# A three-pass down projection, rows loaded by SyncE, and another seam order in a fused decoder layer on one core

## What is computed

```python
x = x + self_attention(layernorm(x))             # 16 heads, window of 64
x = x + cross_attention(layernorm(x), ctx)       # 16 heads, relative bias
xf = layernorm(x)
probs = softmax(xf @ router_w.T); topv, topi = top_k(probs, 2)
g = einsum('nd,edf->nef', xf, gate_w) + gate_b   # F = 512
u = einsum('nd,edf->nef', xf, up_w) + up_b
h = silu(g) * u
y = einsum('ne,ned->nd', probs, einsum('nef,efd->ned', h, down_w) + down_b)
x = x + y
```

## Time and profile before

| | |
|---|---|
| median of 3 runs (lowest to highest) | 1213.61 us (1212.24 to 1214.14) |
| the profiled execution's own time | 1211.85 us |
| its span, first to last instruction | 1210.2 us |
| mean granted TensorE clock | 0.989 |
| busy: PE, DVE, ACT, POOL | 97%, 72%, 62%, 68% of the span |
| DMA | 86.11 MB, mean 71 GB/s |

### The profile page before, as it was taken

How to read it: one execution, slowest core, us unless ns; L and a number is a source line. 1 busy time by engine, 2 the same in 40 slices (tenths; PEclk the granted TensorE clock), 3 DMA queues, 4 the chain that set the end, 5 groups by cost and what they waited for, 6 DMA issues and landing times.

```text
span 1210.2 us, 36900 instructions
## 1 busy us (share of the span) xinstructions
PE 1168.2 (97%) x12874; PEld 1023.7 (85%) x12874; DVE 868.3 (72%) x3851; ACT 753.8 (62%) x1845; POOL 821.0 (68%) x1593
## 2 busy tenths in 40 slices
PE   6899999999999999999999999999899999999996
PEld 4688888888888888888888888887689999998995
DVE  3567888888888888888888888888777655544442
ACT  2567766767766767766766766766564555555552
POOL 4677788778788778788778788876636644444432
PEclk8999999999999999999999999999899999999998
DMA  8411122121122121112112112122765433333221
GB/s 191 93 43 47 50 59 75 50 58 58 51 58 75 50 58 58 51 59 75 52 58 59 51 58 71 48 65 87 230 212 140 76 57 54 53 58 56 46 32 23
DMA packets 70936, 86.11 MB, mean 71 GB/s; under 512 B 25600, under 2 KB 57728, under 8 KB 70752
## 3 DMA queue, kind: packets, MB, share of 16 engines
q1 hardware_dynamic: 54768, 58.60, 16.7%
q0 software_dynamic: 15552, 25.05, 10.7%
q10 hardware_dynamic: 432, 0.10, 0.0%
HBM read 43.10 MB, written 20.95 MB: 53 GB/s over the span
## 4 chain that ended last, share of the span: by engine, by line
PE 90%; DVE 4%; issue 2%; POOL 2%; DMA 1%; ACT 0%; POOLq 0%; DVEq 0%
PE bank_S L901 10%; PE bank_Q L824 7%; PE bank_P L824 6%; PE bank_Q L916 5%; PE bank_S L815 5%; PE bank_S L866 5%; PE bank_B L737 4%; PE bank_A L737 4%; PE bank_B L837 4%; PE bank_A L837 3%; PE bank_A L804 3%; PE bank_P L763 3%; PE bank_B L804 3%; PE bank_Q L876 3%; PE bank_B L796 3%; PE bank_S L754 3%
## 5 line engine op out<-in xcount | busy, mean ns | idle before, releaser
L628 POOL TENSOR_SCALAR arena<-arena,mC 112x375 f32<-112x375 f32 x512 | 297.6, 594 | 26.4 <-DVE mC L1282 24.3
L1282 DVE CUSTOM_DVE_ANT_0 arena<-bank_S,arena 112x375 f32<-112x375 f32 x512 | 260.4, 543 | 56.9 <-PE bank_P L824 30.4
L634 POOL TENSOR_SCALAR arena<-arena 112x112 f32<-112x112 f32 x512 | 175.0, 356 | 85.3 <-DVE arena L1270 85.3
L654 POOL DMA_INDIRECT out<-y,xb x63 | 106.6, 1692 | 83.8 <-DVE y L1420 48.6
L824 PE MATMUL bank_Q<-ident,arena 112*126 112x112 f32 x858 | 131.9, 262 | 2.1 <-POOL arena L628 1.5
L1071 ACT ACTIVATE pTC<-bank_P 126x336 f32<-126x336 f32 x226 | 102.6, 454 | 40.6 <-PE bank_P L824 16.9
L1270 DVE CUSTOM_DVE_ANT_0 arena<-bank_S,arena 112x112 f32<-112x112 f32 x512 | 102.1, 270 | 14.6 <-PE bank_S L754 14.6
L1071 ACT ACTIVATE pTC<-bank_Q 126x336 f32<-126x336 f32 x222 | 101.3, 456 | 18.1 <-PE bank_Q L824 14.6
L824 PEld LDWEIGHTS bank_Q<-ident,arena 112*126 112x126 f32 x858 | 96.2, 141 | 15.4 <-issue 9.7
L824 PE MATMUL bank_P<-ident,arena 112*126 112x112 f32 x678 | 107.9, 268 | 1.3 <-ACT pTC L1071 0.8
L647 POOL DMA_DIRECT2D xb<-xs x63 | 44.1, 700 | 80.1 <-issue 76.6
(11 more groups left out here) (263 smaller groups left out, 3566.9 us busy)
## 6 DMA issues: line engine op xcount, KB each, us to landing
arena<-in_l_ctxT SPq DMA_DIRECT2D x32, 378.0 KB, 3.5
k<-k_low SPq DMA_DIRECT2D x64, 188.0 KB, 2.3
xb<-xs POOLq DMA_DIRECT2D x63, 129.0 KB
q<-q SPq DMA_DIRECT2D x64, 112.0 KB
arena<-in_L_ffn_gate_w SPq DMA_DIRECT2D x8, 512.0 KB
arena<-in_L_ffn_up_w SPq DMA_DIRECT2D x8, 512.0 KB
arena<-in_L_ffn_down_w SPq DMA_DIRECT2D x8, 512.0 KB
arena<-in_x SPq DMA_DIRECT2D x32, 112.0 KB, 2.0
```

Source lines behind the costliest of these rows:

```text
L628: pool.tensor_scalar(z[n % NZ][:, 0:T], z[n % NZ][:, 0:T], -1.0, mC[:, n:n + 1], ALU.mult, ALU.add).then_inc(s_u, 1)
L634: m = pool.tensor_scalar(sF[r][:, j, :], sF[r][:, j, :], -1.0, mF[:, r, j:j + 1], ALU.mult, ALU.add)
L654: pool.indirect_dma_start(out=out[:, :], out_offset=bass.IndirectOffsetOnAxis(ap=xb[x][:, D + 1:D + 2].bitcast(I32), axis=0), in_=y2[x % 2 ...
L1282: dve.tensor_tensor_reduce(out=z[n % NZ][:, 0:T], in0=bank[f"S{r}"][0:S, 0:T], in1=nbias[:, n, :], scale=1.0, scalar=3.0e38, op0=ALU.add, ...
```

## The change

The down projection of the pairs is now done in three passes of fp32r. ScalarE makes the high parts of the hidden rows (`hidden_high`) and of the down weights (`weights_high(..., "dw", ...)`) ahead of silu in step `bg`, VectorE the low parts (`hidden_low`, `weights_low`) at the end of its part of `bg`. `hidden_rows` has one buffer instead of two, `xb` 10 instead of 12. The weighted sums of a pair go alternately into `y2` and `xbT`, so there are four buffers for them up to the last three pairs. The rows of all blocks are loaded by SP (`load_rows`, `load_behind`), not by POOL. In `TAIL_ORDER` only packages 0 to 3 stand at the head, packages 4 to 15 behind the `get` steps, of which there are 8 instead of 10; the parts of the block table come earlier, and `pv3 oc3` ahead of `x3T x3Tc`.

```diff
-XB = 12
+XB = 10
...
 TAIL_ORDER = """
-pkg:0 pkg:1 pkg:2 pkg:3 pkg:4 pkg:5 pkg:6 pkg:7 pkg:8 pkg:9 v0 ln3:-2 t14:-1 st:-2 rs3:-2 t13:-1 p8:-1 v0c
...
-p10 u14 rcA:-2 e10 p9 get:0 u15 e9 p14 u13 x3:-1 pv1 get:1 u12 get:2 get:3 get:4 get:5 get:6 get:7 get:8 get:9
-p15 e14 warm pv2 oc1 e15 p13 oc2 p12 e13 pf:-2 e12 pkg:10 pkg:11 pkg:12 pkg:13 pkg:14 pkg:15 pfD:-2 rcB:-2
-x3T:-1 x3Tc:-1 pv3 oc3 bt otc nrmc rt:-1 lg:-1 re:-1 sc:-2 bg:0 bt:1 onC oncc rcA:-1 bu:0 woc bg:1 st x2 ln3 rs3
...
+pkg:0 pkg:1 pkg:2 pkg:3 v0 ln3:-2 t14:-1 st:-2 rs3:-2 t13:-1 blocks:0 p8:-1 v0c p11:-1 t12:-1 pv0:-1 t15:-1
...
+e6 u10 st:-1 ln3:-1 p8 u9 p11 t14 pv0 rs3:-1 t13 t12 e8 oc0 t15 e11 p10 u14 rcA:-2 e10 p9 get:0 get:1 u15 e9 p14
+u13 x3:-1 pv1 get:2 get:3 u12 get:4 get:5 get:6 get:7 p15 e14 warm pv2 oc1 e15 p13 oc2 p12 e13 pf:-2 e12 pkg:4
+pkg:5 pkg:6 pkg:7 pkg:8 pkg:9 pkg:10 pkg:11 pkg:12 pkg:13 pkg:14 pkg:15 pfD:-2 rcB:-2 pv3 oc3 x3T:-1 x3Tc:-1 bt
+otc nrmc rt:-1 lg:-1 re:-1 sc:-2 bg:0 bt:1 onC oncc rcA:-1 bu:0 woc bg:1 st x2 ln3 rs3 pf:-1 pfD:-1 rcB:-1 sc:-1
+bu:1 x3 x3T x3Tc bg:2 add:0 add:1 rt lg re bu:2 rcA bg:3 add:2 add:3 pf pfD rcB sc blocks:5 bu:3 blocks:6 bg:4
...
-                  for w, n, m in (("gw", DC, F), ("uw", DC, F))}
+                  for w, n, m in (("gw", DC, F), ("uw", DC, F), ("dw", FC, D))}
+            hR = [sb(f"hR_{part}", [P, FC, 2 * P], F32R, st) for part in ("high", "low")]
+            rows_out = [[y2[h] if k % 2 == 0 or k > NP - 4 else xbT[h] for h in range(2)] for k in range(NP)]
...
@@ SP
+                    def load_rows(j):
+                        r = sp.value_load(blocks[0:1, 0, j:j + 1], min_val=0, max_val=E * R)
+                        sp.dma_start(xb[j % XB][:, :], xs[bass.ds(r, P), :]).then_inc(s_xb[j % XB], 16)
+
+                    def load_behind(j):
+
+                        if j:
+                            sp.wait_ge(s_add, 16 * (j - (j > NFULL)))
+                        for n in (j + XB - 2, j + XB - 1) if j < NFULL else (j + XB - 2,):
...
+                            if n < NBLK:
+                                load_rows(n)
...
+                        elif step == "get":
+                            if b == 0:
+                                sp.wait_ge(s_blocks, 1)
+                                buffers_free(sp)
...
+                            load_rows(b)
+                        elif step == "add" and b % 2 == 0:
+                            load_behind(b)
...
@@ PE
                     def down_pair(k):
-                        e = expert_of(pe, 2 * k)
-                        pe.wait_ge(s_hh, 2 * k + 2)
+                        pe.wait_ge(s_dw, k + 1)
+                        pe.wait_ge(s_hl, k + 1)
                         if k:
                             pe.wait_ge(s_yw, 2 * k)
-                        w = package(e, "dw").rearrange("p (c d) -> p c d", c=FC)
                         for h in range(2):
                             for c in range(FC):
-                                m = pe.matmul(bankY[:, h * D:(h + 1) * D], hidden_rows[k % 2][:, c, h * P:(h + 1) * P], w[:, c, :],
-                                              start=(c == 0), stop=(c == FC - 1))
+                                for u, w in PASSES:
+                                    m = pe.matmul(bankY[:, h * D:(h + 1) * D], hR[u][:, c, h * P:(h + 1) * P],
+                                                  wR["dw"][w][:, c, :], start=(c == 0 and (u, w) == PASSES[0]),
...
@@ ACT
+                    def hidden_high(k):
+                        act.wait_ge(s_hh, 2 * k + 2)
+                        if k:
+                            act.wait_ge(s_y, 2 * k)
+                        act.activation(hR[0][:, :, :], hidden_rows[:, :, :], ACT.Copy).then_inc(s_hi, 1)
...
                         elif step == "bg":
...
+                            if b:
+                                hidden_high(b - 1)
+                                weights_high(b - 1, "dw", s_y)
                             for half in range(2):
                                 silu_pair(b, half)
...
@@ DVE
+                        if j >= NFULL:
+                            dve.wait_ge(s_add, 16 * max(j - 1, NFULL))
+                        elif j // 2 > NP - 3:
+                            dve.wait_ge(s_add, 16 * (j - j % 2))
+                        elif j >= 4:
+                            dve.wait_ge(s_add, 16 * (j - j % 2 - 2))
...
+                    def hidden_low(k):
+                        dve.wait_ge(s_hi, k + 1)
+                        dve.tensor_tensor(hR[1][:, :, :], hidden_rows[:, :, :], hR[0][:, :, :].bitcast(F32),
+                                          ALU.subtract).then_inc(s_hl, 1)
...
+                            if b:
+                                hidden_low(b - 1)
+                                weights_low(b - 1, "dw", s_dw, 1)
```

More of the change, by code:

```diff
@@ L518, in load_bias @@
                             sp.dma_start(nbias[s0:s0 + SK, HG * g:HG * (g + 1), :], skewed).then_inc(s_nb[g], 16)
+                    def load_rows(j):
[5 more added lines that the diff above has]
+                        for n in (j + XB - 2, j + XB - 1) if j < NFULL else (j + XB - 2,):
+                            if n == 2 * NP1:
+                                sp.wait_ge(s_blocks, 2)
+                                for q in range(2):
+                                    need(sp, s_st[q], 16 * (B // 2))
+                                    need(sp, s_sc[q], 32 * (B // 2))
+                            if n == NFULL:
+                                sp.wait_ge(s_blocks, 3)
+                                sp.wait_ge(s_pad, 16 * E)
+                                sp.wait_ge(s_spare, 16)
+                            if n < NBLK:
+                                load_rows(n)
                     load_x(0)
@@ L583, in _ @@
                             load_package(sp, e, half)
+                        elif step == "get":
+                            if b == 0:
+                                sp.wait_ge(s_blocks, 1)
+                                buffers_free(sp)
+                                for q in range(2):
+                                    need(sp, s_sc[q], 32 * ((B1 + 1 - q) // 2))
+                                    need(sp, s_st[q], 16 * ((B1 + 1 - q) // 2))
+                            load_rows(b)
+                        elif step == "add" and b % 2 == 0:
+                            load_behind(b)
+                    for j in range(1 + max(b for step, b in steps if step == "add"), NBLK):
+                        if j >= NFULL or j % 2 == 0:
+                            load_behind(j)
                     sp.wait_ge(s_add, 16 * NBLK)
@@ L643, in scatter @@
                                 in_=x3[b % 2][k][:, :], in_offset=None).then_inc(s_sc[b % 2], 16)
-                    def load(j, x):
-                        r = pool.value_load(blocks[0:1, 0, j:j + 1], min_val=0, max_val=E * R)
-                        pool.dma_start(xb[x][:, :], xs[bass.ds(r, P), :]).then_inc(s_xb[x], 16)
                     def add(j, x):
@@ L700, in _ @@
                             scatter(b)
-                        elif step == "get":
-                            if b == 0:
-                                pool.wait_ge(s_blocks, 1)
-                                buffers_free(pool)
-                                for q in range(2):
-                                    need(pool, s_sc[q], 32 * ((B1 + 1 - q) // 2))
-                                    need(pool, s_st[q], 16 * ((B1 + 1 - q) // 2))
-                            load(b, b)
                         elif step == "add":
-                            add_and_load(b)
+                            add(b, b % XB)
                         elif step == "pad":
@@ L1119, in weights_high @@
                             act.wait_ge(used, 2 * k)
-                        act.activation(wR[part][0][:, :, :], package(e, part).rearrange("p (c f) -> p c f", c=DC), ACT.Copy).then_inc(s_wh[part], 1)
+                        act.activation(wR[part][0][:, :, :], package(e, part).rearrange("p (c f) -> p c f", f=parts[part][1] // (
+                            FC if part == "dw" else DC)), ACT.Copy).then_inc(s_wh[part], 1)
                     def silu_pair(k, half):
@@ L1430, in weights_low @@
                         dve.wait_ge(s_wh[part], k + 1)
-                        dve.tensor_tensor(wR[part][1][:, :, :], package(e, part).rearrange("p (c f) -> p c f", c=DC), wR[part][0][:, :, :].bitcast(F32), ALU.subtract).then_inc(then, n)
+                        dve.tensor_tensor(wR[part][1][:, :, :], package(e, part).rearrange("p (c f) -> p c f", f=parts[part][1] // (
+                            FC if part == "dw" else DC)), wR[part][0][:, :, :].bitcast(F32), ALU.subtract).then_inc(then, n)
                     def hidden_pair(k, half):
```

78 lines of the change are left out of this document (31 added, 47 removed).

## The result

The changed kernel takes **1236.67 us** in the median of 4 runs (1235.67 to 1240.66), the kernel before, beside it, 1213.88 (1212.24 to 1218.78): a ratio of 1.0187, 95% interval 1.015 to 1.0225. It is slower by 22.8 us. The forecast was 12.6 us slower, so it had the sign and the largest term's mechanism, but the time lies outside its range of 1214 to 1233.

The account below looks back on a forecast made before the run. PE's own work and few waits were taken as the bound; +24.5 (rows late) + 2.7 (clock) - 11.1 (down) - 1.7 - 1.8 (sum buffers, loads off POOL) = +12.6 us, so 1226.2 us, range 1214 to 1233.

Parts of the forecast that it names:

- Loads on SP: Pair 4's transposes on PE wait for blocks 8 and 9, loaded on SP behind package 15, until 926: +24.5 us.
- SP is through at 866: SP's eight gets, starting after the x2 store at 857.5, are done at 866 (861 to 867).
- the seam's other order: The new order of steps before the pairs, costed at nothing because the wait ahead of pair 4 swallows it.
- The split on ACT and DVE: Each pair's two copies on ACT and two subtractions on DVE fit the 9.07 us period, 0.4 us spare: costed at nothing.
- Down, 19 x 0.585 = -11.1: Down projection on PE takes 2.88 instead of 3.46 us in pairs 2 to 20, those behind the wait: -11.1 us.
- The clock, +2.7: PE starts at the lower clock after the wait ahead of pair 4, slowing transposes and gate: +2.7 us.
- Four buffers for sums: PE's waits of 0.49 and 1.24 us before up go (-1.7), and 1.77 us at the single blocks' start (-1.8).
- by 0.1 us or so: At the end of the pairs, the last pair's four split instructions fit beside gate and up of block 42.
- SP did not get through in time: Rival: SP lands blocks 8 and 9 before PE wants them at about 900, giving 1197.8 us; chance 0.10.
- The passes did not come closer together: Rival: down's 24 matmuls on PE take 2.60 us, 0.28 less per pair, giving 1220.9 us; chance 0.02.
- ACT and DVE become the bound: Rival: the pairs' period stays at 9.65 us, so the 11.1 us are not gained: 1237.3 us; chance 0.05.
- no idle over 5 us, or a period over 9.3: Sign of a wrong prediction: no PE idle over 5 us after 870, or a period over 9.3 us.

Follow-up runs that it names:

- Run 10: Changed kernel with only block table parts 5 to 14 spread over pairs 3 to 16, SP still loading all rows: 1230.61 us, ratio 1.0135.
- run 7: Run 5 with the down projection of the pairs back in float32, without the three passes and their splits: 1212.33 us, ratio 0.9976.
- run 9: Run 6 with the down projections of pairs 0 to 3 left in float32, three passes from pair 4 on: 1203.22 us, ratio 0.9908.
- run 5: Changed kernel with rows of the first 16 blocks loaded by POOL, later ones by SP, and the block table spread: 1209.72 us, ratio 0.996.
- run 6: Run 5 with four buffers for sums to the very end, using wo: 1205.97 us, ratio 0.9927.
- run 4: Changed kernel with all row loads back on POOL and block table parts 5 to 14 spread over pairs 3 to 16: 1219.34 us, ratio 1.0028.
- Run 8: Run 5 with the seam order (`TAIL_ORDER`) of the kernel before, table parts still spread: 1208.38 us, ratio 0.9941.

## Why the prediction failed in size

The span grew by 25.4 us where 12.6 were forecast. By the table above, 5.3 us of the missing 12.8 lie in the wait for rows, 5.5 from T(4) to T(20), 2.9 at the start of the single blocks, less 0.8 behind it.

**Loads on SP: mechanism right, size short by 5.3 us.** PE waited 29.62 us for block 8 behind package 15, and the run with ten loads moved the wait to pair 5 as that reading says. The term was +24.5 and measured +29.8. The step that was short is "SP is through at 866"; it was through at 869.7. Of these 3.7 us, 2.3 are the store, through at 859.8 and not at 857.5: DVE finished that x2 at 859.4 and not at 856.8, since a part of the block table (2.5 us, 856.5 to 859.1) now stands ahead of it. I had costed the seam's other order at nothing since the wait would swallow it, but it lies on the path that ends the wait. The other 1.4 are the time before the first load; between one load and the next SP was at POOL's price (1.17 and 1.15 us). Then the chain of packages was 55.7 us and not 55, the landing came 5.1 us after package 15 went out, as counted, and PE started 0.6 us after it.

**The split on ACT and DVE costed at nothing: wrong, and the largest error, 6.4 us.** The timetable was right for the steady stretch (DVE waits 0.7 us for the sums where 0.4 were worked out, ACT in time, period 9.07, down 2.88). But rows 5 and 6, from which DVE's room was read, lie at 957 to 963 and 1000 to 1010, where the kernel before has no table parts on DVE. In pairs 4 to 8 DVE also has two parts of the block table in a pair, and ahead of them the router of the last sequences. I had named a thin cover and priced 0.1 us over it at 1.9 us, but had not asked what else lies in the cover. Run 10 gives the table parts alone 6 us; runs 7 and 9 give the first pairs 4.7 and 3.7 us, and in the changed kernel the latter were swallowed by the long wait. From T(4) to T(20) the terms now add up: +6.4 (table), +2.2 (clock), -9.3 (16 downs) and -2.3 (the two waits of before and the slower starts behind them) make -3.0, where -2.9 was measured.

**Down, 19 x 0.585 = -11.1:** right where it could show. The 24 matmuls take 2.88 us; runs 5 and 7 differ by 8.0 us over 14 pairs, 0.57 each. The Trainium skill's single gap (TensorE: Matmul & The Clock Gate, "Back-to-back issue gap") would, as an estimate, have made them 2.62; the trace does not agree, with 2.88 in every steady period.

**The clock, +2.7:** right. The transposes took 1.09 and the gate 4.38 us after the wait, against 0.44 and 2.87 once warm: +2.2, at a granted clock of 0.61 in 920 to 940.

**Four buffers for sums: the first part misread, the second short by 2.9 us.** The -1.7 is in the second line of that table of differences. Of its two waits the 0.49 was the adds, but the 1.24 was mostly a table part on DVE, as its rows above show; I had blamed the adds for both, and so passed over the one sign in the old trace of what the table would do. At the end the -1.8, and 1.8 for the last three downs, came to -0.7 together. PE waited 0.69, 0.37 and 1.24 us for sums there. By run 6 the last two are buffers (the sums of pairs 18 to 20 and of the single blocks still share y2), the first is the last pair's own chain (hidden high 1103.08, low 1104.17, down weights low 1105.31, sums 1106.44), which has no up of a next pair beside it. I had let it fit "by 0.1 us or so".

**The rivals.** SP did not get through in time. The passes did not come closer together. That ACT and DVE become the bound was the rival nearest to the largest error: I had taken it for all pairs or none, and it held for five. The upper end of the range allowed 1 to 2 us for late ACT or DVE, and the table parts cost 6.4. My sign that the prediction would be wrong, "no idle over 5 us, or a period over 9.3", did half its work: the period was 10.35 from T(5) to T(10) and 9.07 later.

**What the change would need.** Its parts are worth something once none is in the other's way: the early loads on POOL, the late ones on SP, the table spread, four buffers to the end and the passes only from pair 4 on give 1203.2 us, by the ratios 34 less than the changed kernel and 11 less than the one before. What was not tried is packages and loads interleaved on SP alone; package waits stand in SP's order, and a pair whose expert is the last would wait for a package behind a load that waits for that pair.

## What to carry to other kernels

A transfer that is moved to another queue takes over everything that stands waiting ahead of it there: count those waits, and the time at which each can begin, not only the first of them. When work is moved onto an engine with "room", make the timetable for every stretch in which it will run, not for the quietest one; small instructions of another job that hid in the same gap are the first to surface. And where a faster engine shortens the period, look for the loops on other engines that are just shorter than the old one (POOL's 9.18 us here, between 9.07 and 9.65).

## What the runs showed of the hardware

- A load whose address comes from a register cost SP 1.17 us of its queue from one to the next (eight from 861.18 to 869.72 in the changed kernel), where a plain package issue took 0.37 to 0.51. POOL needed about the same, 1.18 us in run 4 (1059.74 to 1060.92) and 1.15 in the earlier trace rows.
- In run 5 PE waited 1.71 us up to 910.48, and the granted clock was 0.50 in 912 to 914, back at 1.00 from 916. In run 8 it waited 2.74 us up to 893.86, and the clock was 0.56 to 0.58 in 894 to 898. A wait of 1.7 us can so cost about twice itself. It need not: in the changed kernel a wait of 1.95 us up to 881.41 and those of 0.67 to 1.32 in pairs 4 to 8 left the clock at 1.00.
- An add into `out` took POOL between 1.6 and 2.6 us. In the steady stretch of the changed kernel it was this, with DVE busy 15.22 of 18 us in 1010 to 1028:

```profile
1059.20 2.13 POOL L690 DMA_INDIRECT out<-y,xb  x1 [4.07 <-DVE y L1438]
1061.63 2.56 POOL L690 DMA_INDIRECT out<-y,xb  x1 [0.30 <-issue]
```

  In run 4, with DVE busy 16.15 of 18 us in 1010 to 1028, the adds at 1024.88 and 1026.83 took 1.65 and 1.57; in the kernel before, with DVE at 10.79 of 18, those at 1011.35 and 1013.82 took 2.17 and 1.59. So it is not DVE's load; what makes the difference was not tried.
